# Attention state of 64 columns, and its products in four strips of TensorE's array, in a fused AdaLN block with linear attention and a mixture of experts

## The reference

```python
h = layernorm(x) * (1 + ca) + sa
# attention: 16 heads of 16
q, k, v = h @ Wq, h @ Wk, h @ Wv
gk = log_sigmoid(h @ Wgk1 @ Wgk2 + bgk2) / 16
def step(state, inp):                       # one token after the other
    qt, kt, vt, gt = inp
    gate = exp(gt)                          # (heads, 16)
    state = state * gate[..., None] + vt[..., None] * kt[..., None, :]
    out_t = einsum('bhvk,bhk->bhv', state, qt)
out = layernorm(outs) * gamma + beta
x = x + ga * ((out * silu(h @ Wg)) @ Wout)
# experts: 8, the best 2 of each token
h = layernorm(x) * (1 + cb) + sb
x = x + gb * moe(h)
```

## Time and profile before

| | |
|---|---|
| median of 3 runs | 936.38 us (936.37 to 936.99) |
| profiled execution, and its span | 936.14 us, 934.4 us |
| PE busy | 827.2 us (89%) |
| DVE busy | 671.4 us (72%) |
| ACT busy | 442.4 us (47%) |
| POOL busy | 348.4 us (37%) |
| chain that ended last | PE 39%, DVE 36%, issue 16%, DVEq 3% |

### The profile page before, as it was taken

How to read it: one execution, slowest core, us unless ns; L and a number is a source line. 1 busy time by engine, 2 the same in 40 slices (tenths; PEclk the granted TensorE clock), 3 DMA queues, 4 the chain that set the end, 5 groups by cost and what they waited for, 6 DMA issues and landing times.

```text
span 934.4 us, 23154 instructions
## 1 busy us (share of the span) xinstructions
PE 827.2 (89%) x6879; PEld 726.3 (78%) x6880; DVE 671.4 (72%) x1561; ACT 442.4 (47%) x1167; POOL 348.4 (37%) x403
## 2 busy tenths in 40 slices
PE   4799899888989898989509999999999999999995
PEld 4566666666666676667309999999999999999995
DVE  2468888888888888887745686768677685775953
ACT  1476666666766666666304333333333324333330
POOL 5124443443344434434210242525234243253342
PEclk9799999999999999999758999999999999999998
DMA  6401111111111111111170252534325243223232
GB/s 231 177 19 59 47 49 49 58 46 54 44 58 46 58 41 58 52 52 42 42 256 2 48 138 48 134 50 129 54 43 139 46 112 67 38 40 50 40 43 32
DMA packets 53190, 65.14 MB, mean 70 GB/s; under 512 B 5826, under 2 KB 48660, under 8 KB 53012
## 3 DMA queue, kind: packets, MB, share of 16 engines
q1 hardware_dynamic: 28820, 35.02, 11.5%
q0 software_dynamic: 13440, 18.36, 11.3%
q10 hardware_dynamic: 10880, 11.14, 4.3%
HBM read 39.47 MB, written 25.03 MB: 69 GB/s over the span
## 4 chain that ended last, share of the span: by engine, by line
PE 39%; DVE 36%; issue 16%; DVEq 3%; DMA 2%; ACT 2%; SPq 1%; POOL 0%; ACTq 0%; POOLq 0%
PE p_a L1146 17%; PE p_cum L1146 8%; DVE w_hi L917 5%; DVE acts_r L1110 5%; PE p_gz L1146 4%; PE p_qk L1146 4%; PE p_v L1146 4%; DVE w_parts L946 2%; PE p_qk L1165 1%; DVE st L849 1%; DVE host_o L929 1%; DVE x L974 1%; DVE st_x L849 1%; DVE st_o L1029 1%; PE p_a L1316 1%
## 5 line engine op out<-in xcount | busy, mean ns | idle before, releaser
L655 POOL DMA_INDIRECT out_dram<-host_n,tok x72 | 121.5, 1688 | 299.7 <-DVE host_n L1130 285.5
L1146 PE MATMUL p_a<-w_hi_r,acts_r 128*128 x1152 | 211.2, 282 | 5.3 <-DVE host_n L1130 5.3
L1146 PEld LDWEIGHTS p_a<-w_hi_r,acts_r 128*128 128x128 f32 x1152 | 179.1, 188 | 6.6 <-issue 6.5
L1146 PE MATMUL p_a<-w_lo_r,acts_r 128*128 x576 | 161.9, 281 | 0.0
L1110 DVE CAST acts_r<-acts 128x2048 fp32r<-128x2048 f32 x36 | 74.0, 2057 | 64.3 <-ACT acts L798 64.3
L807 ACT ACTIVATE x_host<-p_a,mods 128x256 f32<-128x256 f32 x72 | 36.7, 561 | 175.6 <-PE p_a L1316 168.4
L1146 PEld LDWEIGHTS p_a<-w_lo_r,acts_r 128*128 128x128 f32 x576 | 108.5, 188 | 0.0
L609 POOL TENSOR_TENSOR ln_host<-w_parts,gam 128x256 f32<-128x256 f32 x32 | 23.1, 721 | 187.7 <-DVE w_parts L964 187.7
L1112 DVE TENSOR_TENSOR acts_r<-acts,acts_r 128x2048 fp32r<-128x2048 f32 x36 | 82.5, 2293 | 1.2
L634 POOL DMA_INDIRECT expert_rows<-rows,pos x64 | 63.7, 996 | 49.7 <-issue 32.4
L917 DVE TENSOR_TENSOR w_hi<-p_a,upto 128x1024 f32<-128x1024 f32 x64 | 75.2, 1217 | 3.2 <-PE p_a L1146 3.0
(11 more groups left out here) (214 smaller groups left out, 1825.4 us busy)
## 6 DMA issues: line engine op xcount, KB each, us to landing
w<-in_L_ffn_W_dram SPq DMA_DIRECT2D x16, 1024.0 KB, 7.5
ln_host<-expert_rows ACTq DMA_DIRECT2D x36, 272.0 KB, 3.3
host_x<-in_L_attn_x_dram SPq DMA_DIRECT2D x64, 128.0 KB, 2.1
out_dram<-x SPq DMA_DIRECT2D x32, 128.0 KB, 1.7
acts<-in_L_wmod_dram SPq DMA_DIRECT2D x1, 1536.0 KB, 6.7
out_dram<-host_n,tok POOLq DMA_INDIRECT x72, 4.1
expert_rows<-pad_rows ACTq DMA_DIRECT2D x4, 272.0 KB, 3.7
expert_rows<-pad_rows SPq DMA_DIRECT2D x4, 272.0 KB, 4.4
```

Of the source, the lines that this page charges most:

```text
L655: nc.gpsimd.indirect_dma_start(out=out, out_offset=bass.IndirectOffsetOnAxis(ap=tok[u][:, h:h + 1], axis=0), in_=y_out[u][:, h, :], in_off ...
L1146: return nc.tensor.matmul(dst, lhsT, rhs, start=start, stop=stop, skip_group_check=True)
```

## The change

- `state`, `state_sum`, `state_end`, `decay` and `e_tot` have 64 columns in place of 256: for a quarter b of block j the 32 partitions of b hold their 32 x 32 square in the columns j * 32 to j * 32 + 31.
- The decay's mask is `parity` (one column per head of a pair) in place of `own`, in one instruction in place of two.
- The sum over the chunk, the product `p_u` and the product of state and queries are each written as 32-wide pieces: 8 products for the sum, 8 for `p_u`, 4 for each block's state part. Piece b writes the partitions b * 32 to b * 32 + 31.
- Inside the loop PE's three waits ahead of the output block become waits by themselves, with their values put in registers first.

```diff
-        p_u, p_ot = p_cum[:, 0:D], p_cum[:, D:2 * D]
+        p_u, p_ot = p_cum[:, 0:KD * 2 * HD], p_cum[:, D:2 * D]
...
+        SC = KD * 2 * HD
+        state, state_sum = state[:, 0:SC], state_sum[:, 0:SC]
...
-        e_tot = in_w2.take(D)
-        decay = [in_w1.take(D) for i in range(2)]
-        state_end = in_w2.take(D)
+        e_tot = in_w2.take(SC)
+        decay = [in_w1.take(SC) for i in range(2)]
+        state_end = in_w2.take(SC)
...
-                    for j in range(KD):
-                        last = nc.gpsimd.tensor_tensor(
-                            decay[v][:, j * P:(j + 1) * P].rearrange("p (h d) -> p h d", d=HD),
-                            e_tot[:, j * P:(j + 1) * P].rearrange("p (h d) -> p h d", d=HD),
-                            own[:].unsqueeze(2).to_broadcast([P, HB, HD]), ALU.mult)
-                    last.then_inc(decay_ready, 1)
+                    nc.gpsimd.tensor_tensor(
+                        decay[v].rearrange("p (j k d) -> p j k d", k=2, d=HD),
+                        e_tot.rearrange("p (j k d) -> p j k d", k=2, d=HD),
+                        parity[:].unsqueeze(1).unsqueeze(3).to_broadcast([P, KD, 2, HD]), ALU.mult).then_inc(decay_ready, 1)
...
-                    A.activation(e_tot[:], p_cum[:, D:2 * D], ACT.Exp, scale=q / 2)
+                    A.activation(e_tot[:], p_cum[:, D:D + SC], ACT.Exp, scale=q / 2)
...
-                    mm(p_oT[:, j * P:(j + 1) * P], state[:, j * P:(j + 1) * P], qkT[u][:, j, :], True, False)
+                    for b in range(QUADS):
+                        rows_b = slice(b * 32, (b + 1) * 32)
+                        mm(p_oT[rows_b, j * P:(j + 1) * P], state[rows_b, j * 32:(j + 1) * 32], qkT[u][rows_b, j, :], True, False)
...
-                    for n, sums in enumerate((upto_half, ones)):
-                        last = mm(p_cum[:, n * D:(n + 1) * D], sums[:], log_gz[:, D:2 * D], True, True)
+                    mm(p_cum[:, 0:D], upto_half[:], log_gz[:, D:2 * D], True, True)
+                    for j in range(KD):
+                        for b in range(QUADS):
+                            at = D + j * P + b * 32
+                            last = mm(p_cum[b * 32:(b + 1) * 32, D + j * 32:D + (j + 1) * 32], ones[:, 0:32],
+                                      log_gz[:, at:at + 32], True, True)
...
-                    after(pe, state_ready, s)
-                    pe.wait_ge(vn_ready, s + 1)
-                    pe.wait_ge(am_ready, KD * (s + 1))
+                    if isinstance(s, int):
+                        after(pe, state_ready, s)
+                        pe.wait_ge(vn_ready, s + 1)
+                        pe.wait_ge(am_ready, KD * (s + 1))
+                    else:
+                        wait_apart(pe, (state_ready, s), (vn_ready, s + 1), (am_ready, KD * (s + 1)))
...
-                    for j in range(KD):
-                        last = mm(p_u[:, j * P:(j + 1) * P], qk[u][:, D + j * P:D + (j + 1) * P],
-                                  vn[u][:, j * QUADS:(j + 1) * QUADS], True, True)
+                    for j in range(KD):
+                        for b in range(QUADS):
+                            at = D + j * P + b * 32
+                            last = mm(p_u[b * 32:(b + 1) * 32, j * 32:(j + 1) * 32], qk[u][:, at:at + 32],
+                                      vn[u][:, j * QUADS + b], True, True)
```

## The result

| | before | after |
|---|---|---|
| median | 936.38 us | 925.32 us (924.94 to 927.36, 4 runs) |
| ratio | 1 | 0.9892, 95% interval 0.9879 to 0.9906 |
| profiled execution, span | 936.14, 934.4 us | 925.61, 923.8 us |
| DVE, POOL busy | 671.4, 348.4 us | 659.3, 310.2 us |

The kernel is 11.1 us faster; the forecast was 929.5, 6.8 us less in the profiled execution, which came out 10.5 less. The direction and the mechanism held, and the two gains that were forecast came to 0.01 us a step. The cost at the score was about half of what was taken, and the sum lacked one term.

The account below looks back on a forecast made before the run. A ring of DVE work and PE's piece from `log_gz` to the score was taken to bound the attention loop. 8.4 us won less 1.6 at the score gave 6.8 us less, 929.5 us, range 924.5 to 936.

Parts of the forecast that it names:

- The ring: Attention loop, 32 steps of about 13.1 us: DVE work, PE from `log_gz` to the score, DVE work again.
- `state_sum`, 0.20 us in both kinds of step: DVE's L1006, 256 to 64 columns: 417 to 214 ns, so output transposes and `o_tok` come 0.20 us earlier in odd steps.
- `pick` in the even step: DVE's `pick`, 0.73 us beside POOL's L624 in 48% of steps, is released earlier; PE's transposes become the limit, gain 0.37 us.
- The `hT` way: Second ring, from `rows` through ACT to `l_gz`: slack 0.44 us less 0.07 for the signal lets even steps win 0.37.
- `ones`, +0.05 at the score: PE's gate total as 8 products of 32 columns: score 0.05 us later per step, bounds -0.10 and +0.35.
- DVE. Only `state_sum` shrinks: On DVE only `state_sum` was to shorten, by 0.20 us, bounds 0.26 and nothing.
- The sum: Some 30 steps: 8.4 us won, 1.6 given back at the score over 32 steps, leaving 6.8 and a forecast of 929.5.
- the forecast's own range: Times of 926 to 932 us, inside the wider stated range of 924.5 to 936.
- A: Rival, slower: the state's four strips share one PSUM bank and go one behind the other, 0.86 us a block; 942.5; chance 0.09.
- B: Rival: short strip passes cost like long ones, +0.35 us at the score; 938.9, halfway near 934; chance 0.15.
- C: Rival: only the odd gain, as `hT` holds even steps or POOL holds another DVE operation than `pick`; 933.5; chance 0.11.
- D: Rival: the score comes 0.05 us earlier instead of later; 926.1; chance 0.65 together with the forecast.

Follow-up runs that it names:

- router_first: Changed kernel with PE's router product moved ahead of the cumulative sums, into PE's wait for `log_gz`: 904.89 us, ratio 0.9664.
- sum_wide: Changed kernel with DVE's `state_sum` over 256 columns again, POOL and PE left narrow: 934.45 us, ratio 0.9982.
- pool_wide: Changed kernel with POOL's two state products (L624, L626) over 256 columns again, all else at 64: 928.09 us, ratio 0.9912.
- decay_two: Changed kernel with POOL's decay as two products of 128 columns again, half of them used: 929.03 us, ratio 0.9926.
- before_again: The kernel before, unchanged, run for a second trace: 934.83 us in one execution.
- ones4: Changed kernel with the gate's total as four products of 64 columns in place of eight of 32: 923.81 us, ratio 0.9865.
- pe_only: Changed kernel with `state_sum`, both state products and the decay over 256 columns again, leaving PE's strips, ACT's shorter `e_tot` and the seam: 943.79 us, ratio 1.0088.

## Why the prediction was right, and where its sum was short

**What bounds the kernel.** Right. The ring of DVE's work and of PE's piece up to the score is shown by `router_first`, and the table of distances says where the change touched it.

**`state_sum`, 0.20 us in both kinds of step.** Right: 218 ns for 214 forecast, 0.199 in the odd step, and `sum_wide` took back 0.20 in both.

**`pick` in the even step, with PE as the new limit, together 0.37.** Right: 0.365, of which 0.014 are lost again ahead of the masks. `pool_wide` took back 0.16 (0.17). `pick` itself was to stay below 0.3 and takes 0.32, because POOL's 64 columns cost 323 ns for 230. The forecast had drawn its line through the state product and the decay, two products that differ in one operand. The higher price stayed without effect, since `pick` was no longer what released `o_tok`: DVE waits for PE there in all of 28 steps, up from 14 of 27.

**The `hT` way, just enough slack.** Right: the distance from the masks to `log_gz` didn't move in either kind of step.

**`ones`, +0.05 at the score.** The term was mis-sized: +0.028, smaller than taken by 0.7 us in 32 steps. The strips' passes do cost by columns, and the router's open weights are the 0.10 that were put in; the allowance of 0.05 for passes that follow less closely was too much by half.

**The missing term.** The step that failed was "DVE. Only `state_sum` shrinks". The decay was costed at nothing, as work of a queue that waits anyway. It lay beside `rows`, which is on the ring, and held it up by 0.06 us, 1.8 us in 30 steps; `decay_two` shows it. The kernel before had the sign of it: the same operation on the same shape takes 413 ns as `host_n` and 476 as `rows`. The forecast had seen POOL hold up `pick` and looked for no second place among the instructions ahead of it.

**The sum.** Per pair of steps the ring is 0.379 + 0.225 shorter, so 0.30 a step, where the forecast's terms made 0.28 - 0.05. Some 29 steps of it make 8.8, and the three behind the last `log_gz` give 0.8 more (30.9 us to the last score, then 30.1). From the first score to the last the trace is 9.3 us shorter (399.0 to 389.7), and that is what the change is worth by the steps. Against the 6.8 of the forecast, 1.8 are the missing term and 0.7 the score's; the count of 30 steps was short by about one.

**Luck.** Of the 10.5 us in the profiled execution 1.2 more lie outside that stretch, where nothing was won: 1.4 behind the last score, less 0.1 ahead of the first, both within the scatter that `before_again` shows. Without them the time would have been near 927, inside the forecast's own range. The interval of the ratio, 8.8 to 11.3 us less, holds both.

**The rivals.** A (strips in one PSUM bank go one behind the other) is out: eight passes in four strips of 32 rows, all into the same bank, took 0.35 us with their emptying, where 0.86 were priced. The rule of the Trainium skill, "TensorEngine Tiling (Array Packing)", section on PSUM pressure, does not hold up these strips, each of which writes partitions of its own. B is out by `ones4` and the 0.27 of the group. C, in its second form, was true the other way round: POOL holds up another operation of DVE than `pick`, but before the change and not after. D's time (926.1) is nearer to the measured one than the forecast's, yet its mechanism is out: the score comes 0.028 us later, not 0.05 earlier. What no rival had was PE's clock: the trace of the whole change shows no fall in the loop, two variants that keep only a part of it (`pe_only`, `sum_wide`) do.

**Not tried**: PE's strips with the three waits in the loop as they were before; the filled and the unfilled variants on one chip; a trace of the slower pair of `decay_two`.

## What to carry to other kernels

When a kernel has a ring through two engines, write down its pieces as distances between starts of the same instructions, and compare these, not busy shares: a change of 0.03 us a step is then visible that no median shows (the median of `ones4` pointed to the wrong theory). An operation on a queue that waits anyway isn't free while it runs beside an engine that is on the ring: look for one operation that has two durations on one shape. And move whatever PE can do early into its waits on the ring; that was worth 20 us here, twice the change itself.

## What the runs showed of the hardware

- A group of 16 short passes in four strips (32 columns each, fp32) takes 0.27 us with its emptying, and 0.25 as eight of 64 columns. Going into strips costs 0.08 to 0.09 us between the groups, coming out of them by estimate about as much (0.27 less 0.12 of streaming and 0.03 of weights), and the next full-width weights are not loaded ahead (their load starts with the product at 250.31, where before it started 0.21 us ahead; the router's group took 0.46 for 0.36).
- POOL's state product takes 727 ns on 256 columns and 323 on 64, its decay 395 ns on 128 and 292 on 64: a straight line through 727 and 395 gives 230 for 64 columns, too little for either.
- DVE's fp32 scaling of 256 columns from SBUF to SBUF (`rows`), with one tile as input, is held up beside POOL too: 476 ns for 413, with 0.32 us of the decay left to run when it starts.
- TensorE's granted clock fell to half for 3.4 us, five times, in the middle of a loop in which it is busy for 88% of the time (`pe_only`), and each time a step lost 1.4 us by it. With two products of no use in each step no fall was left, on another chip (943.8 to 936.5 us). Less work for PE can make a kernel slower.
